# Starting the last attention's first batch inside the feed-forward

## The reference

```python
x = x + L0_xattn(layernorm(x), ctx)   # 12 heads of 64, q and k normalised
x = x + L0_ffn(layernorm(x))
#   h = silu(x @ w1.T * s1) * (x @ w2.T * s2)     256 -> 1024, gated
#   h = gelu(h @ h1.T * t1); h = gelu(h @ h2.T * t2)   1024 -> 1024, twice
#   y = h @ w3.T * s3                             1024 -> 256
x = x + L1_xattn(layernorm(x), ctx, mask)   # 16 heads of 16 over 64 keys
#   softmax(q k.T / 4, masked) v, then @ Wo.T + bo
x = x + L1_moe(layernorm(x))          # top 1 of 8 experts, 256 -> 1024 -> 256
```

## Time and profile before

| | us |
|---|---|
| median of 3 runs | 795.4 |
| the profiled execution: its time | 798.0 |
| its span, first to last instruction | 796.1 |
| PE (TensorE matmul) busy | 745.0 (94%) |
| DVE (VectorE) busy | 460.0 (58%) |
| ACT (ScalarE) busy | 248.4 (31%) |
| POOL (GpSimd) busy | 183.4 (23%) |
| granted TensorE clock, mean | 0.982 of full |

### The profile page before, as it was taken

One profiled execution on the slowest core, in us unless ns is written; L12 is line 12 of the kernel. 1 busy time (PEld: TensorE's weight loads), 2 busy tenths in 40 slices (PEclk: granted clock), 3 DMA queues, 4 the chain that ended last, 5 costly groups with the idle time before them and its releaser, 6 DMA issues.

```text
span 796.1 us, 11304 instructions
## 1 busy us (share of the span) xinstructions
PE 745.0 (94%) x4168; PEld 578.6 (73%) x4168; DVE 460.0 (58%) x897; ACT 248.4 (31%) x455; POOL 183.4 (23%) x183
## 2 busy tenths in 40 slices
PE   5999899989999999999999999998987699999995
PEld 3676576768878888888888888775554597777674
DVE  4646479888982584348424943289798742333331
ACT  3425133132311132123222321256566232223221
POOL 3012134461020002000200020056564222222221
PEclk9979999999999999999999999999999899999998
DMA  9970800002300000000000000019013878899950
GB/s 326 383 254 2 369 1 0 1 1 80 134 2 2 2 2 2 2 2 2 2 2 2 2 2 2 2 25 412 1 54 107 275 268 312 259 282 302 310 159 7
DMA packets 21726, 86.64 MB, mean 109 GB/s; under 512 B 3229, under 2 KB 12384, under 8 KB 16352
## 3 DMA queue, kind: packets, MB, share of 16 engines
q1 hardware_dynamic: 19088, 78.18, 27.8%
q0 software_dynamic: 2560, 7.34, 2.7%
HBM read 79.22 MB, written 18.35 MB: 123 GB/s over the span
## 4 chain that ended last, share of the span: by engine, by line
PE 79%; DVE 13%; issue 4%; DMA 1%; ACT 1%; POOL 1%; SPq 0%; DVEq 0%; POOLq 0%
PE ps L1178 37%; PE ps L2177 8%; PE ps L2150 6%; PE ps L593 5%; PE ps L544 4%; PE ps L2142 3%; PE ps L1331 2%; PE ps L530 2%; DVE any_bits L357 2%; DVE head_max L1787 1%; PE ps L622 1%; DVE head_sum L1796 1%; PE ps L538 1%; DMA xs<-rows,token_in 1%; PE ps L1543 1%
## 5 line engine op out<-in xcount | busy, mean ns | idle before, releaser
L1256 ACT ACTIVATE f_raw<-ps,cols 128x512 f32<-128x512 f32 x96 | 66.2, 690 | 242.1 <-PE ps L1178 219.4
L1178 PE MATMUL ps<-f_ha_hi,fh 128*128 128x512 f32 x256 | 99.9, 390 | 1.6 <-DVE inexact L377 1.5
L1178 PE MATMUL ps<-f_hb_hi,fh 128*128 128x512 f32 x256 | 100.1, 391 | 0.0
L1178 PE MATMUL ps<-f_ha_lo,fh 128*128 128x512 f32 x256 | 99.6, 389 | 0.0
L1178 PE MATMUL ps<-f_hb_lo,fh 128*128 128x512 f32 x256 | 99.6, 389 | 0.0
L1279 DVE CAST f_ha_hi<-f_raw 128x512 fp32r<-128x512 f32 x64 | 27.6, 432 | 84.9 <-ACT f_raw L1256 83.9
L2177 PE MATMUL ps<-ew,hT 128*128 (+1 forms) x320 | 72.7, 381 | 2.3 <-ACT hT L2230 1.8
L2177 PEld LDWEIGHTS ps<-ew,hT 128*128 128x128 f32 (+1 forms) x320 | 52.5, 169 | 16.5 <-issue 4.4
L1178 PEld LDWEIGHTS ps<-f_ha_hi,fh 128*128 128x128 f32 x256 | 48.1, 188 | 12.3 <-issue 2.4
L1178 PEld LDWEIGHTS ps<-f_hb_lo,fh 128*128 128x128 f32 x256 | 48.1, 188 | 10.2 <-issue 0.2
L1178 PEld LDWEIGHTS ps<-f_hb_hi,fh 128*128 128x128 f32 x256 | 48.1, 188 | 10.2 <-issue 0.2
(11 more groups left out here) (322 smaller groups left out, 1362.3 us busy)
## 6 DMA issues: line engine op xcount, KB each, us to landing
ew<-in_ew SPq DMA_DIRECT2D x27, 1028.0 KB, 6.8
fh<-fh_copy SPq DMA_DIRECT2D x2, 4096.0 KB, 14.9
ew<-in_ew SPq DMA_DIRECT2D x1, 8192.0 KB, 22.3
b_rows<-in_eb SPq DMA_DIRECT2D x14, 256.0 KB
fw<-fw_copy SPq DMA_DIRECT2D x3, 1024.0 KB, 6.9
x_res<-in_x SPq DMA_DIRECT2D x4, 512.0 KB, 10.6
rows<-x_res SPq DMA_DIRECT2D x4, 512.0 KB, 3.5
rows<-xn_e SPq DMA_DIRECT2D x4, 512.0 KB, 3.0
```

The source lines that it names most:

```text
L1178: ins = nc.tensor.matmul(out, *((xk, wk) if swap else (wk, xk)), start=(k == 0 and part == 0), stop=(k == w.shape[1] - 1 and part == 1))
L1256: nc.scalar.activation(f_raw[:, m % 3, :], ps[:, ring_bank(n), :], ACT.Silu if m < KH else ACT.Gelu, scale=col(("w1_s", "h1_s", "h2_s")[m ...
```

## The change

1. Columns(0) and queries(0) move from the fourth layer's products 3 and 5 to the third layer's products 5 and 7. Keys of batch 0 get a buffer of their own (`k_first`), built after the third layer's products; keys of batch 1 are built after the fourth's.
2. scores(0,0) and scores(0,1) stand behind the fourth layer's products 6 and 7, scores(0,2) and scores(0,3) behind the output products of tiles 2 and 3. All four write banks 0 and 1, so each waits until `subtract_max` has read the one before.
3. On VectorE, subtract_max(0,0) and (0,1) stand behind the splits of the last two hidden tiles, subtract_max(0,2) and (0,3) behind output tiles 2 and 3, and invert_sum(0,j) behind each output tile j.
4. On TensorE, before gate_part(0) stands a wait for all four of batch 0's subtractions (banks 0 and 1). fold moves behind scores(1,0).
5. On GpSimd, the four divisions of batch 0 stand ahead of the last feed-forward statistics; `bo1_wide` is made before them. On ScalarE, two exponentials stand before the rows of batch 1 and two behind.
6. The DMA of `wo1n` starts after the third layer; the 8 MB DMA of the experts' second weights `ew2` starts when batch 0's probabilities are transposed (its region now holds `c_first`), not after batch 0's scores.
7. In the gated layer of all four batches the cast to `hi` moves from VectorE to ScalarE (`gated_high`), one tile late; VectorE keeps the multiplication and the subtraction (`gated_low`), also one tile late.

```diff
+        def score_bank(b, j):
+            return 0 if b == 0 else 2 + 2 * (j % 2)
...
                 if i == LAST:
                     attn1_keys(pool, 0)
+                    pool.tensor_copy(bo1_wide[:], ...).then_inc(consts_ready, 1)
                     attn1_keys(pool, 1)
+                    for j in range(TT):
+                        attn1_divide(pool, 0, j)
                 after(pool, f_var, i, TT, TT)
                 keep_moments(pool, i, f_norm)
...
-                        if w is fh2 and i == LAST and o == 3:
+                        if w is fh1 and i == LAST and o == KH - 3:
                             after(pe, f_in, B, 2, 2)
                             attn1_columns(pe, 0)
-                        if w is fh2 and i == LAST and o == 5:
+                        if w is fh1 and i == LAST and o == KH - 1:
                             attn1_queries(pe, 0)
+                        if w is fh2 and i == LAST and o >= KH - 2:
+                            attn1_scores(pe, 0, o - KH + 2)
...
                             f_mm_full, swap=True)
+                    if i == LAST:
+                        attn1_scores(pe, 0, j)
+
+        def gated_high(act, i, o):
+            after(act, f_up_taken, i, KH, o + 1)
+            nc.scalar.activation(f_ha[0][:, o, :], f_raw[:, o % 3, :], ACT.Identity).then_inc(f_hi, 1)
...
+                    if i == LAST and m >= 3 * KH - 2:
+                        attn1_subtract_max(dve, s_order, 0, m - 3 * KH + 2)
...
                     add_eps(j).then_inc(f_var, 1)
+                    if i == LAST and j >= 2:
+                        attn1_subtract_max(dve, s_order, 0, j)
+                    if i == LAST:
+                        attn1_invert_sum(dve, s_order, 0, j)
...
+        def attn1_scores(pe, b, j):
+            n = b * TT + j
+            if j == 0:
+                pe.wait_ge(c_q_out, NG1 * (b + 1))
+                pe.wait_ge(c_keys, NG1 * (b + 1))
+            if b == 0:
+                if j:
+                    pe.wait_ge(c_sub, j)
...
-            sp.wait_ge(c_s_full, TT)
+            sp.wait_ge(c_pT_full, PAIRS1)
             sp.dma_start(ew2[:], ew2_d.rearrange("e p k n -> p e k n")).then_inc(ld_ew, 16)
...
             for b in range(B):
-                scores(b, 0)
-                scores(b, 1)
+                if b == 0:
+                    pe.wait_ge(c_sub, TT)
+                else:
+                    attn1_scores(pe, b, 0)
+                    if b == 1:
+                        fold()
+                    attn1_scores(pe, b, 1)
                 gate_part(pe, b)
                 if b < LAST:
                     attn1_columns(pe, b + 1)
```

More of the change, by code:

```diff
@@ L1274, in ffn_vector @@
                                                        ALU.mult, ALU.mult).then_inc(f_up_taken, 1)
-                        after(dve, f_up_taken, i, KH, o + 1)
+                        if o:
+                            gated_low(o - 1)
+                        if o == KH - 1:
+                            gated_low(o)
                     else:
                         after(dve, f_act_out, i, F_HID, m + 1)
-                    hi, lo = (part[:, o, :] for part in (f_hb if m // KH == 1 else f_ha))
-                    order.step(nc.vector.tensor_copy(hi, raw))
-                    nc.vector.tensor_tensor(lo, raw, hi.bitcast(F32), ALU.subtract).then_inc(f_split, 1)
+                        hi, lo = (part[:, o, :] for part in (f_hb if m // KH == 1 else f_ha))
+                        order.step(nc.vector.tensor_copy(hi, raw))
+                        nc.vector.tensor_tensor(lo, raw, hi.bitcast(F32), ALU.subtract).then_inc(f_split, 1)
+                    if i == LAST and m >= 3 * KH - 2:
+                        attn1_subtract_max(dve, s_order, 0, m - 3 * KH + 2)
                     if m == KH - 1 and i == 0:
@@ L1299, in ffn_vector @@
                     add_eps(j).then_inc(f_var, 1)
+                    if i == LAST and j >= 2:
+                        attn1_subtract_max(dve, s_order, 0, j)
+                    if i == LAST:
+                        attn1_invert_sum(dve, s_order, 0, j)
                 order.end()
+        def attn1_scores(pe, b, j):
[6 more added lines that the diff above has]
+                    pe.wait_ge(c_sub, j)
+            elif n == TT:
+                after(pe, f_act_out, LAST, F_HID, F_HID)
+            elif n == TT + 1:
+                after(pe, f_y_taken, LAST, TT, TT - 1 + 2)
+            else:
+                pe.wait_ge(c_sub, n - 1)
+            halves = [(ps[:, score_bank(b, j) + r, :], slice(r * KEYS, (r + 1) * KEYS)) for r in range(2)]
+            for o in range(NG1):
+                for bank, half in halves:
+                    nc.tensor.matmul(bank[:, o * D:(o + 1) * D], first_or(c_qT, b)[half, o, j * P:(j + 1) * P],
+                                     keys_of(b)[half, o].rearrange("p g k -> p (g k)"),
+                                     start=(o == 0), stop=False)
+            for bank, half in halves:
+                ins = nc.tensor.matmul(bank, fillT[half, j * P:(j + 1) * P],
+                                       each_key[half].rearrange("p g k -> p (g k)"), start=False, stop=True)
+            ins.then_inc(c_s_full, 1)
@@ new lines, in attn1_subtract_max @@
+        def attn1_subtract_max(dve, order, b, j):
+            dve.wait_ge(c_s_full, TT * b + j + 1)
+            if b >= 2:
+                dve.wait_ge(c_pT_full, PAIRS1 * (b - 1))
+            first = score_bank(b, j)
+            logits = ps[:, first:first + 2, :].rearrange("p o (g k) -> p (o g) k", k=KEYS)
+            top_ = head_max[:, j, :]
+            order.step(nc.vector.tensor_reduce(top_, logits, AX.X, ALU.max))
+            nc.vector.tensor_tensor(tokens_of(b)[:, j], logits, top_.unsqueeze(2).broadcast_to([P, H1, KEYS]),
+                                    ALU.subtract).then_inc(c_sub, 1)
@@ L1303, in attn1_columns, with attn1_invert_sum @@
+        def attn1_invert_sum(dve, order, b, j):
+            dve.wait_ge(c_exp, TT * b + j + 1)
+            if b:
+                dve.wait_ge(c_prob, TT * (b - 1) + j + 1)
+            sums = head_sum[:, j, :]
+            order.step(nc.vector.tensor_reduce(sums, tokens_of(b)[:, j], AX.X, ALU.add))
+            nc.vector.reciprocal(sums, sums).then_inc(c_inv, 1)
         def attn1_columns(pe, b):
@@ L1480, in attn1_gpsimd @@
                         pool.memset(first[:, :, 0:E], 0.0).then_inc(consts_ready, 1)
-                for j in range(TT):
-                    divide(b, j)
+                if b:
+                    for j in range(TT):
+                        attn1_divide(pool, b, j)
                 if b == 2:
@@ L1592, in fold @@
                 pe.wait_ge(consts_ready, 1)
+                after(pe, f_y_taken, LAST, TT, 2 * TT - 1)
                 for m in range(KD):
@@ L1653, in attn1_tensor @@
                     attn1_queries(pe, b + 1)
-                scores(b, 2)
-                if b >= 1:
+                if b:
+                    attn1_scores(pe, b, 2)
                     probabilities(b - 1, 0, 2)
-                scores(b, 3)
-                if b == 0:
-                    fold()
-                if b >= 1:
+                    attn1_scores(pe, b, 3)
                     probabilities(b - 1, 2, 2)
@@ L1845, in logits, with subtract_max, invert_sum @@
                 g_order.step(nc.vector.tensor_tensor(e, raw, by_expert(row("gate_b", E), TT), ALU.add))
-            for b in range(B):
+            def subtract_max(b, j):
+                attn1_subtract_max(dve, s_order, b, j)
+            def invert_sum(b, j):
+                attn1_invert_sum(dve, s_order, b, j)
+            for b in range(1, B):
                 subtract_max(b, 0)
```

119 lines of the change are left out of this document (51 added, 68 removed).

## The result

The changed kernel is slower: median 810.3 us (807.7 to 814.1, 6 runs) beside 795.9 (795.4 to 799.0, 6 runs) of the kernel before on the same chip, ratio 1.018 [1.0157, 1.0204], so 14.4 us. Predicted were 807.7, with a range of 801.5 to 811.5. The profiled execution took 807.7 with a span of 805.8.

A forecast was written before the change was run, and what follows sets the result against it. It took TensorE's back-to-back matmuls, then VectorE's queue from the output products on, as the bound. +13.8 us for the delayed batch 1 and -1.5 for the flag gave +12.3 on 795.4: 807.7, range 801.5 to 811.5.

The forecast's parts named there:

- The fourth subtraction holds gate_part(0): Last feed-forward batch: gate_part(0) waits for VectorE's fourth batch-0 subtraction, ending at 544.9; it had started at 526.97.
- Additions: VectorE's additions to x_res for tiles 1 to 3, blocked beside GpSimd divisions: 1.45 us each, 4.35 in all.
- Exponential wait: VectorE idles before invert 2, right behind subtract_max(0,2), for ScalarE's exponential: 1.2 us.
- gate_part, columns and eviction: TensorE after the wait: these take 3.66 us at the low clock instead of 2.41.
- Queries: Batch 1's queries on TensorE, behind the columns: 3.6 us, the clock taken to be back.
- rival 2: Low clock lasts through all eight query matmuls of batch 1: 3.6 us more, 811.3 in total; chance 0.09.
- scores(1,0) to scores(1,1): Batch 1 on TensorE: a score group of 1.18 us, then fold of 1.88; from 552.9 to 556.0.
- The stretch: Up to subtract_max(1,2): it starts at 564.6 instead of 550.75, +13.8 us, carried whole to the end.
- The flag: First feed-forward batch: cast on ScalarE brings VectorE's bit check 2.2 us earlier, ending TensorE's flag wait: -1.5, bounds 0 and -1.7.
- GpSimd's statistics, ew2's DMA, batches 2 and 3: Later statistics and the later ew2 transfer cost 0; batches 2 and 3 shift as a whole.
- rival 4: Slack on VectorE in batches 2 and 3 wins back up to 8 us: near 799; chance 0.07.
- Rival 3: Batch-0 softmax hidden after all, batch 1 starting 2.4 us earlier: 791.5 if the fourth subtraction ends before 533; chance 0.04.

The follow-up runs named there:

- the run without gaps: Changed kernel plus filler matmuls: nine before scores(0,3), eight before gate_part(0), one between columns(1) and queries(1); 810.5 us, ratio 1.0155.
- the cast alone: Kernel before with only the gated layer's cast to hi moved to ScalarE, one tile late; 795.9 us, ratio 1.0.
- the banks: Changed kernel with scores(0,2) and (0,3) in banks 2 to 5, gate_part(0) waiting for two subtractions; 810.1 us, ratio 1.0172.
- banks and exponentials: Changed kernel with scores(0,2), (0,3) in banks 2 to 5 and ScalarE's third and fourth exponentials behind batch 1's gate, columns and query evictions; 799.2 us, ratio 1.0044.
- the one with the row sums late: Changed kernel with separate banks, later exponentials, row sums of tiles 2 and 3 behind the fourth subtraction, divisions early; 795.4 us, ratio 0.999.
- banks, exponentials, row sums late and divisions late: Changed kernel with separate banks, later exponentials, late row sums of tiles 2 and 3, GpSimd divisions behind the last statistics; 792.7 us, ratio 0.9965.

## Why the prediction was right

Each step, from the first output product of each trace and with the two inserted score groups counted in at the 2.36 of the prediction:

- *The fourth subtraction holds gate_part(0).* Predicted 544.9, so 28.05 behind the hidden layers' end at 516.85; measured 539.03 - 513.40 + 2.36 = 27.99. The named releaser is VectorE, as said.
- *Its parts.* Additions: 1.53 each, three times (1.95 - 0.42), predicted 1.45. Exponential wait: 1.12, predicted 1.2. The two score groups ahead of the output products were mis-sized: 2.86 instead of 2.36, so that the fourth subtraction really stands 28.5 behind the hidden layers' end. Nothing is left over for the columns and queries of batch 0, as predicted.
- *gate_part, columns and eviction*: 542.70 - 539.03 = 3.67, predicted 3.66, at half clock.
- *Queries*: predicted 3.6, measured 5.66. This is the term that was mis-sized, by 2.1 us. It is half of rival 2: the sum took it that gate part and columns would be enough to bring the clock back, as in the earlier trace rows, and gave 0.09 to the case that it stays low for all eight, at 811.3. It stayed low for somewhat over half of them: 1.96 more than 3.70, where all eight would be 3.6 more. In the traces of the other kernels that still wait, the queries took 5.85, 5.99, 6.02, 6.24 and 6.37. The mechanism is the predicted one, and the run without gaps showed its size. By its time alone (810.3) the change would have spoken for rival 2 (811.3) rather than for the sum (807.7); only the trace tells that the clock came back half way.
- *scores(1,0) to scores(1,1)*, with fold between: 552.29 - 549.13 = 3.16, predicted 3.1. *From there to subtract_max(1,2)*: 561.00 - 552.29 = 8.71, predicted 8.6.
- *The stretch*: +16.1 instead of +13.8. Of the difference, 2.1 is the queries.
- *The flag*: VectorE reached the bit check 2.6 earlier (206.82 - 189.84 = 16.98 against 213.54 - 193.98 = 19.56), predicted 2.2, and TensorE no longer idles. This term was mis-sized too: the cast alone took 2.17 out of the feed-forward, predicted 1.5 with a bound of 1.7. At the flag itself the gain is 1.65 (two products stood 1.88 apart there and now 0.23); 0.3 came ahead of it, since the third layer's first product starts 14.72 behind the feed-forward's first instead of 15.02. In the table's column 0.5 of the gain is hidden by the score groups, and that the remaining 1.7 meets the bound is luck. That the cast alone did not show as a gain in the times fits with the trace, where two falls of the clock ate it.
- *GpSimd's statistics, ew2's DMA, batches 2 and 3*: nothing, as said. "(1,2) to (2,2)" is 20.89 in both, the rest is within 0.04, and nothing was eaten (rival 4).

Sum 16.1 - 1.7 = +14.4, predicted +12.3. Of the 2.1 between them the queries are +2.1, the score groups +0.5 and the flag -0.7; the last two nearly cancel. Rival 3 (hidden after all) failed at the point that was named for it: it wanted the fourth subtraction before 533, so within 16.2 us of the hidden layers' end, and it took 28.0. TensorE idled 7.96 + 5.78 = 13.7 us before gate_part(0), where 10 or more were named, and VectorE 8.91 before subtract_max(1,0), where some 7 were.

Where I fell short is the remedy that follows from the text. It blames the wait for four subtractions; taking this wait away from gate_part(0) alone brought nothing, because the same VectorE queue also reached TensorE through ScalarE's order (exponentials ahead of the eviction of `gate_x`). The prediction was right on the time and incomplete on the cause, and only the pair of edits showed it: -0.4 in "into (1,2)" for the banks, -11.3 for banks and exponentials together (some 2 of it the queries, back at full clock). Whether ScalarE's order alone would do was not tried; the wait for four subtractions would then still stand on TensorE.

## What to carry to other kernels

Work moved ahead into a "free" engine brings its own queue with it: before moving softmax tiles into a stretch, write down what on every other engine will stand behind their last step, by way of banks and of the order of evictions, and free all of those ways or none. Put GpSimd's operations on SBUF beside VectorE work that reads PSUM, not beside two-input additions (1.53 us each here). And compare kernels by distances between fixed points of the traces, since whole executions move by several us in stretches that nobody changed (the first attention by 5.2 here).

## What the runs showed of the hardware

- A VectorE addition with two SBUF inputs (128 x 256 float32, 0.42 alone) that starts up to 0.24 us into a GpSimd tensor_tensor of 1.90 took 1.95 or 1.96 in all eleven cases in the traces of four kernels (three each in the changed, the banks and the banks-and-exponentials kernel, two in the one with the row sums late), and ended some 0.28 behind the division where both rows stand here. The maximum and subtraction that read PSUM beside a division kept their 1.22. By the Trainium skill (SBUF — State Buffer, "Who interferes with whom") such an instruction is blocked and not slowed; the trace agrees, with the end of the addition just behind the end of the division.
- Filling TensorE's wait did not keep the clock where the filling stopped before the release: full until a little past 541, then 0.50 through the queries, with gaps of 1.59 and 0.69. With both gaps closed it stayed at 1.00; which of the two gaps matters was not separated. With a gap of 0.7 ahead of the queries the clock stayed full in the banks-and-exponentials kernel (queries in 3.70 at 526.54).
- The clock also fell with hardly a longer gap than that. In the kernel with banks, exponentials, row sums late and divisions late TensorE had not stood idle for over 0.78 us at a time since the output products, and yet the clock is 0.50 from about 539.3 on, behind scores(1,0) and fold:

```profile
536.02 1.13 PE L1367 MATMUL ps<-k_blocks,c_qT 64*128 64x256 f32 x8 [0.78 <-ACT c_qT L1434]
...
539.19 1.97 PE L1367 MATMUL ps<-k_blocks,c_qT 64*128 64x256 f32 x8
```

```profile
540.00:542.00 2.00, 2.00 (x20) 0.95 (x22) 1.97 (x2) 0.16 (x3) 2.00 (x2) 0.50 0.00 0
```

So the length of a single gap doesn't tell by itself whether the clock falls; what else does is not shown here.
- The same work behind the same gaps ran at either clock in two traces: scores in 1.14 and 2.08, heads in 1.92 and 3.60, before and in the kernel with the cast alone. Whether the 2.17 us taken out ahead of it, or the execution, made the difference is open.
